# A decoder layer's feed-forward stage: where the vector engine adds a tile's sum, and where it takes the first half's maximum

## The chip, the cores and the metric

The kernel runs on one core of a Trainium2 chip. The core has a matrix engine (TensorE, PE), a vector engine (VectorE, DVE), a scalar engine (ScalarE, ACT), a general engine (GpSimd, POOL) and a queue engine that mostly issues transfers (SyncE, SP). Each engine works through its own list of instructions in order, and the lists meet only through semaphores. The metric is the device time of one execution in microseconds (us), the median of several runs; lower is better.

## What is computed

The program is one decoder layer on 2,048 tokens of width 512: windowed attention, a four-expert mixture that routes by token id, and a feed-forward stage with quantized activations. The change touches the feed-forward stage alone:

```python
def activation_quant(x):                       # per token, 8 bit
    s = 127 / clip(max(abs(x), axis=-1), EPS)
    return clip(round(x * s), -128, 127) / s
def bit_linear(x, w):                          # weight_quant(w): -1, 0 or 1, times mean(abs(w))
    return activation_quant(x) @ weight_quant(w).T
h = silu(bit_linear(x, w_gate)) * bit_linear(x, w_up)     # 2048 columns
h = rms_norm(h, ln_weight)
out = x_residual + bit_linear(h, w_down)                  # x is layernorm(x_residual)
```

## The kernel before, in words

The feed-forward stage, `ffn_phase`, works on 16 tiles of 128 tokens. The 2,048 hidden columns of a tile are four chunks of 512 (c = 0 to 3), and two chunks are a half. For tile t the work is this:

- TensorE, `gate_up(t, c)`: four matmuls into `gate_ps` and four into `up_ps`. Both exist twice and alternate by chunk.
- ScalarE, `gate_of(t, c)`: the silu, `f_gate` from `gate_ps`.
- VectorE, `hidden(t, c)` (line 1606): the h values of the chunk, from `up_ps` and `f_gate`. Here they are called h0 to h3.
- GpSimd, `weighted(t, c)` (line 1473): `hw`, which is h times the norm's weight. Here hw0 to hw3.
- VectorE, `top_of(t, n)` (line 1612): the largest absolute value of a half of `hw` in each row. `top_of(t, 0)` needs hw0 and hw1, `top_of(t, 1)` needs hw2 and hw3.
- ScalarE, `squares(t, n)` (line 1537): sum of squares of a half of h. VectorE `sum_squares` and GpSimd `rms_of` make the norm's factor of it.
- VectorE `scale_h(t)` (lines 1625 to 1634) and `quantize_h(t)` (line 1643, two halves, `hq_big`), then ScalarE `pack(t, 0)` and `pack(t, 1)` (line 1522, `hq`), then SyncE transposes each half by a DMA into `hqT` (line 1429).
- TensorE, `down(t, g)` for g = 0 to 3 (line 1738): four matmuls each, all sixteen adding up in the single buffer `f_y_ps`.
- VectorE, `y_of(t)` (line 1648): scales the finished `f_y_ps` and adds it to the tile's residual. SyncE stores the result and loads a later tile in its place.

These steps are spread over several passes of one loop. In its pass t, TensorE runs `gate_up(t, c)` and behind each of them `down(t - 2, c)`, since `LATE_DOWN` is 2. `down(t, 0)` waits for `y_of(t - 1)`, because `f_y_ps` exists once. `gate_up(t, 3)` waits for h1 of tile t, `gate_up(t + 1, 0)` for h2, `gate_up(t + 1, 1)` for h3. ScalarE's pass t is: second half's squares of tile t - 1, gate 0, normalize tile t + 2, gate 1, copy of the transposed x, pack 0 of tile t - 1, gate 2, pack 1 of tile t - 1, gate 3, first half's squares of tile t. GpSimd's pass t is `rms_of(t - 1)`, hw0, hw1, hw2, `rstd_of(t + 3)`, hw3, and a small scale.

VectorE's pass t, written out by hand at lines 1665 to 1688, is: `mean_of(t + 2)` (line 1580, one short instruction), `y_of(t - 3)`, `top_of(t - 1, 1)`, h0, the norm and quantizer of tile t - 1 with the maximum of x for tile t + 2 between them, h1, h2, `quantize_x(t + 2)`, statistics of tile t + 3 (lines 1568 to 1575), `top_of(t, 0)`, h3. What is left of the last tiles follows the loop.

Of the kernel before, what the change touches and what calls it, by code (L numbers as in the profile page):

```python
# [53 lines left out]
LATE_DOWN = 2  # L54
# [1278 lines left out]
def ffn_phase(nc, io, x2, y, sh):  # L1333
# [4 lines left out]
    with ExitStack() as ctx:  # L1338
# [69 lines left out]
        def inside(t):  # L1408
            return 0 <= t < TILES

        def flat(tile, i):
            return tile[:, i].rearrange("p c n -> p (c n)")

        with nc.Block() as block:
# [149 lines left out]
            def _(dve):  # L1564
                def stats_of(t):
                    i = t % 2
                    dve.wait_ge(x_loaded[t % len(homes)], t // len(homes) * 16 + 16)
                    nc.vector.bn_stats(bn_st[:, i, :], xt[t]).then_inc(stats_step, 1)  # L1568

                def variance_of(t):  # L1570
                    i = t % 2
                    dve.wait_ge(stats_step, t + 1)
                    nc.vector.bn_aggr(bn_mv[:, i, :], bn_st[:, i, :]).then_inc(stats_done, 1)  # L1573
                    dve.wait_ge(stats_done, t + 1)
                    nc.vector.tensor_scalar(var_eps[:, i:i + 1], bn_mv[:, i, 1:2], LN_EPS, None, ALU.add).then_inc(eps_added, 1)

                def mean_of(t):
                    i = t % 2
                    dve.wait_ge(rstd_ready, t + 1)
                    nc.vector.scalar_tensor_tensor(mean_rstd[:, i:i + 1], bn_mv[:, i, 0:1], -1.0, rstd[:, i:i + 1],  # L1580
                                                   ALU.mult, ALU.mult).then_inc(mean_ready, 1)

                def top_of_x(t):
                    dve.wait_ge(xn_ready, t + 1)
                    nc.vector.tensor_reduce(x_max[:], xn[:], AX.X, ALU.max, apply_absolute_value=True).then_inc(xq_step, 1)  # L1585

                def scale_x(t):
                    at = t * XQ_STEPS
                    dve.wait_ge(xq_step, at + 1)
                    if inside(t - 1):  # L1590
                        dve.wait_ge(gu_ready, t)
                    nc.vector.tensor_scalar(x_max127[:], x_max[:], Q_EPS, 1.0 / QMAX, ALU.max, ALU.mult).then_inc(xq_step, 1)  # L1592
                    dve.wait_ge(xq_step, at + 2)
                    nc.vector.reciprocal(x_inv[:], x_max127[:]).then_inc(xq_step, 1)

                def quantize_x(t):
                    dve.wait_ge(xq_step, (t + 1) * XQ_STEPS)
                    if inside(t - 1):
                        dve.wait_ge(xq_transposed, t)
                    nc.vector.tensor_scalar(xq_big[:], xn[:], x_inv[:], CODE, ALU.mult, ALU.add).then_inc(xq_ready, 1)  # L1600

                def hidden(t, c):
                    i = t % 2
                    dve.wait_ge(gate_ready, t * FC + c + 1)
                    dve.wait_ge(up_summed, t * FC + c + 1)
                    nc.vector.scalar_tensor_tensor(h[:, i, c, :], up_ps[c % 2][:], gu_scale[:, i, 1:2], gate[:, c % 2, :],  # L1606
                                                   ALU.mult, ALU.mult).then_inc(h_ready, 1)

                def top_of(t, n):
                    i = t % 2  # L1610
                    dve.wait_ge(hw_ready, t * FC + 2 * n + 2)
                    nc.vector.tensor_reduce(hw_max[:, i, n:n + 1], flat(hw, i)[:, n * HALF:n * HALF + HALF], AX.X, ALU.max,  # L1612
                                            apply_absolute_value=True).then_inc(hw_max_ready, 1)

                def sum_squares(t):
                    dve.wait_ge(sq_ready, (t + 1) * HALVES)
                    nc.vector.tensor_reduce(h_ss[:], h_sq[:, t % 2, :], AX.X, ALU.add).then_inc(ss_ready, 1)
                    dve.wait_ge(ss_ready, t + 1)
                    nc.vector.tensor_scalar(h_var[:], h_ss[:], 1.0 / F, RMS_EPS, ALU.mult, ALU.add).then_inc(h_var_ready, 1)

                def scale_h(t):
                    i = t % 2
                    at = t * HQ_STEPS
                    dve.wait_ge(hw_max_ready, (t + 1) * HALVES)
                    nc.vector.tensor_reduce(h_top[:], hw_max[:, i, :], AX.X, ALU.max).then_inc(hq_step, 1)
                    dve.wait_ge(hq_step, at + 1)
                    dve.wait_ge(rms_ready, t + 1)
                    nc.vector.tensor_scalar(h_max[:], h_top[:], h_rms[:], Q_EPS, ALU.mult, ALU.max).then_inc(hq_step, 1)  # L1628
                    dve.wait_ge(hq_step, at + 2)
                    nc.vector.reciprocal(h_inv[:], h_max[:]).then_inc(hq_step, 1)  # L1630
                    nc.vector.tensor_scalar(y_scale[:, t % (LATE_DOWN + 2):t % (LATE_DOWN + 2) + 1], h_max[:], w_mean[:, 2:3], 1.0 / QMAX, ALU.mult, ALU.mult)\
                        .then_inc(hq_step, 1)
                    dve.wait_ge(hq_step, at + 4)
                    nc.vector.tensor_scalar(h_mul[:], h_inv[:], h_rms[:], QMAX, ALU.mult, ALU.mult).then_inc(hq_step, 1)  # L1634

                def quantize_h(t):
                    i = t % 2
                    dve.wait_ge(hq_step, (t + 1) * HQ_STEPS)
                    for n in range(HALVES):
                        cols = slice(n * HALF, n * HALF + HALF)  # L1640
                        if inside(t - 1):
                            dve.wait_ge(hq_packed, (t - 1) * HALVES + n + 1)
                        nc.vector.tensor_scalar(hq_big[:, cols], flat(hw, i)[:, cols], h_mul[:], CODE, ALU.mult, ALU.add)\  # L1643
                            .then_inc(hq_ready, 1)

                def y_of(t):
                    dve.wait_ge(y_summed, t + 1)
                    nc.vector.scalar_tensor_tensor(xt[t], y_ps[:], y_scale[:, t % (LATE_DOWN + 2):t % (LATE_DOWN + 2) + 1], xt[t],  # L1648
                                                   ALU.mult, ALU.add).then_inc(y_ready, 1)
# [15 lines left out]
                for t in range(TILES):  # L1665
                    if inside(t + 2):
                        mean_of(t + 2)
                    if inside(t - 1 - LATE_DOWN):
                        y_of(t - 1 - LATE_DOWN)
                    if inside(t - 1):  # L1670
                        top_of(t - 1, 1)
                    hidden(t, 0)
                    if inside(t - 1):
                        sum_squares(t - 1)
                    if inside(t + 2):
                        top_of_x(t + 2)
                        scale_x(t + 2)
                    if inside(t - 1):
                        scale_h(t - 1)
                        quantize_h(t - 1)  # L1680
                    hidden(t, 1)
                    hidden(t, 2)
                    if inside(t + 2):
                        quantize_x(t + 2)
                    if inside(t + 3):
                        stats_of(t + 3)
                        variance_of(t + 3)
                    top_of(t, 0)
                    hidden(t, 3)
                last = TILES - 1  # L1690
                y_of(last - LATE_DOWN)
                top_of(last, 1)
                sum_squares(last)
                scale_h(last)
# [125 lines left out]
```

## Time and profile before

| | us |
|---|---|
| median of 3 runs | 809.09 |
| lowest, highest | 807.49, 811.71 |
| the profiled execution's own time | 808.96 |
| its span | 807.1 |
| busy in the span: TensorE | 740.2 |
| VectorE | 590.4 |
| ScalarE | 473.2 |
| GpSimd | 281.0 |

The profiled execution's time is 1.86 us more than its span, which lies around the span. The feed-forward stage begins at about 600 us of the span and ends with it; its first h value starts at 611.4. TensorE's end times are modelled, so its busy time is not a measure of how much room it has. Two starts of an engine's consecutive instructions tell its pace better.

### The profile page before, as it was taken

Reading aid. Unit: us, or ns where it says so; the run is one execution under the profiler, and the core shown is the slowest. Engines: PE = TensorE matmul, PEld = TensorE weight load, DVE = VectorE, ACT = ScalarE, POOL = GpSimd, SP = SyncE. Lnnn points to the kernel's source line nnn. Section 1 sums busy time; section 2 is a strip of 40 time slices with the busy share of each in tenths; the row PEclk is TensorE's granted clock in tenths of the full one; section 3 lists DMA queues with packets and bytes.
Section 4 is the critical chain, followed back from the end, with each engine's and each line's share of the span. In section 5 each row is a group of like instructions: output and inputs, shape, how many; then the busy total and the mean of one; then the engine's idle time right before and its main releaser. Section 6 shows DMA issues by size and latency. Waiting matters only on the chain. (4 is left out here: it accounts for less than half of the span.)

```text
span 807.1 us, 14098 instructions
## 1 busy us (share of the span) xinstructions
PE 740.2 (92%) x5150; PEld 507.8 (63%) x5150; DVE 590.4 (73%) x1092; ACT 473.2 (59%) x1025; POOL 281.0 (35%) x282
## 2 busy tenths in 40 slices
PE   5988999999999999999978789999957899999997
PEld 4756777777777777777655568888833343434443
DVE  6886666877668866677675467778628888888875
ACT  5555676666666666677555144444415766767674
POOL 2011213223042130314455234443214555555552
PEclk9998999999999999999989899999989999999999
DMA  9200031113121040313210375553122232433332
GB/s 312 107 1 28 27 105 37 45 54 131 52 81 54 28 157 27 106 30 129 105 53 2 95 274 176 201 199 137 46 82 85 52 85 73 105 91 73 73 78 79
DMA packets 56482, 74.12 MB, mean 92 GB/s; under 512 B 35615, under 2 KB 37663, under 8 KB 54752
## 3 DMA queue, kind: packets, MB, share of 16 engines
q1 hardware_dynamic: 50672, 56.17, 22.8%
q0 software_dynamic: 5456, 16.53, 5.9%
q8 instruction: 43, 0.70, 0.4%
q10 hardware_dynamic: 288, 0.52, 0.2%
q14 instruction: 23, 0.19, 0.1%
HBM read 52.71 MB, written 13.39 MB: 82 GB/s over the span
## 5 line engine op out<-in xcount | busy, mean ns | idle before, releaser
L527 ACT ACTIVATE probs<-s_ps,neg_max 128x512 f32<-128x512 f32 (+2 forms) x256 | 152.3, 610 | 19.5 <-DVE neg_max L696 18.1
L696 DVE TENSOR_REDUCE neg_max<-s_ps 128x2 f32<-128x1024 f32 (+2 forms) x128 | 124.5, 1014 | 33.6 <-PE s_ps L910 33.0
L930 PE MATMUL pT_ps<-ident,probs 128*128 128x128 f32 x832 | 115.6, 280 | 9.7 <-DVE probs L717 8.4
L539 ACT ACTIVATE probs<-pT_ps 128x512 f32<-128x512 f32 x96 | 57.4, 598 | 98.6 <-PE pT_ps L930 98.3
L930 PEld LDWEIGHTS pT_ps<-ident,probs 128*128 128x128 f32 x832 | 93.9, 144 | 25.2 <-DVE probs L717 11.2
L717 DVE COPY probs<-pT_ps 128x512 f32<-128x512 f32 x112 | 76.6, 684 | 36.8 <-PE pT_ps L930 36.5
L1473 POOL TENSOR_TENSOR hw<-h,ln_w_sb 128x512 f32<-128x512 f32 x64 | 83.2, 1310 | 52.3 <-DVE h L1606 52.3
L1738 PE MATMUL f_y_ps<-w_tern,hqT 128*128 128x512 bf16 x256 | 65.1, 379 | 11.8 <-DVE xn L1648 5.3
L1717 PE MATMUL gate_ps<-w_tern,xqT 128*128 128x512 bf16 x256 | 65.9, 380 | 8.3 <-DVE h L1606 7.4
L843 PE MATMUL side_ps<-w_hi 128*128 128x512 f32 x172 | 71.0, 413 | 0.0
L843 PE MATMUL side_ps<-w_hi,w_lo 128*128 128x512 f32 x172 | 67.3, 391 | 0.0
L843 PE MATMUL side_ps<-w_lo,w_hi 128*128 128x512 f32 x172 | 67.2, 391 | 0.0
L1717 PE MATMUL up_ps<-w_tern,xqT 128*128 128x512 bf16 x256 | 65.7, 379 | 0.0
L399 POOL TENSOR_TENSOR aT_hi<-norm,one_col 128x512 fp32r<-128x512 f32 x15 | 15.6, 1040 | 125.0 <-DVE norm L708 86.6
L1606 DVE SCALAR_TENSOR_TENSOR h<-up_ps,gu_scale,f_gate 128x512 f32<-128x512 f32 x64 | 47.7, 745 | 7.1 <-ACT f_gate L1529 7.0
L527 ACT ACTIVATION_READ_ACCUMULATOR probs<-s_ps,neg_max 128x1 f32 x256 | 52.8, 206 | 0.0
L952 PE MATMUL pv_ps<-probs,v_sb 128*32 128x256 f32 (+1 forms) x896 | 52.3, 369 | 0.2 <-ACT probs L539 0.2
L391 POOL TENSOR_TENSOR norm<-rinv,one_col 128x512 f32<-128x512 f32 x16 | 16.7, 1041 | 102.8 <-DVE rinv L703 102.8
L1717 PEld LDWEIGHTS gate_ps<-w_tern,xqT 128*128 128x128 bf16 x256 | 23.6, 98 | 42.0 <-DVE h L1606 15.4
L1738 PEld LDWEIGHTS f_y_ps<-w_tern,hqT 128*128 128x128 bf16 x256 | 23.2, 97 | 42.0 <-DMA hqT<-hq 18.0
L1522 ACT ACTIVATE hq<-hq_big,minus_offset 128x1024 bf16<-128x1024 f16 x30 | 34.3, 1143 | 25.4 <-DVE hq_big L1643 25.4
L1529 ACT ACTIVATE f_gate<-gate_ps,gu_scale 128x512 f32<-128x512 f32 x64 | 43.1, 674 | 8.2 <-PE gate_ps L1717 8.2
(247 smaller groups left out, 1635.5 us busy)
## 6 DMA issues: line engine op xcount, KB each, us to landing
w_piece<-w_ffn SPq DMA_DIRECT2D x24, 512.0 KB
w_stage<-w_ffn SPq DMA_DIRECT2D x12, 1024.0 KB
xres<-x POOLq DMA_DIRECT2D x4, 1024.0 KB, 5.7
xn<-x SPq DMA_DIRECT2D x12, 256.0 KB, 3.0
xn<-x SPq DMA_DIRECT2D x3, 1024.0 KB
x<-xres POOLq DMA_DIRECT2D x3, 1024.0 KB, 4.8
xn<-c SPq DMA_DIRECT2D x2, 1024.0 KB, 6.1
v_next<-c SPq DMA_DIRECT2D x2, 1024.0 KB, 6.0
```

The lines of the kernel that those rows point to most:

```text
L527: nc.scalar.activation(weights[qt][:, h, at:at + width(qt)], s_ps[:, h, 0:width(qt)], ACT.Exp, bias=neg_max[:, qt % 2, h:h + 1], accum_out ...
L539: nc.scalar.activation(out, turned_p, ACT.Identity).then_inc(slot_copied[0], 1)
L696: nc.vector.tensor_reduce(neg_max[:, qt % 2, 2 * s:2 * s + 2], s_ps[:, 2 * s:2 * s + 2, 0:width(qt)], AX.X, ALU.max, negate=True).then_inc ...
L717: nc.vector.tensor_copy(weights[qt][:, :, a:z], pT_ps[:, 1, :].rearrange("p (h n) -> p h n", h=GH))\
L843: last = nc.tensor.matmul(out, lt, r, start=(first and n == 0), stop=(final and n == len(terms) - 1))
L930: last = nc.tensor.transpose(pT_ps[:, k % 2, h * P:h * P + P], weights[qt][:, h, a:z], ident[:])
L952: last = nc.tensor.matmul(pv_ps[HD * h:HD * h + HD, to], v_sb[:, slot, f:f + HD], p, start=first, stop=final, tile_position=(0, HD * h))
L1473: nc.gpsimd.tensor_tensor(hw[:, t % 2, c, :], h[:, t % 2, c, :], ln_w[:, c * CHK:c * CHK + CHK], ALU.mult)\
L1529: nc.scalar.activation(gate[:, c % 2, :], gate_ps[c % 2][:], ACT.Silu, scale=gu_scale[:, t % 2, 0:1])\
L1606: nc.vector.scalar_tensor_tensor(h[:, i, c, :], up_ps[c % 2][:], gu_scale[:, i, 1:2], gate[:, c % 2, :], ALU.mult, ALU.mult).then_inc(h_re ...
L1717: last = nc.tensor.matmul(out[:], xqT[:, t % 2, k, :], weights[:, k, cols], start=(k == 0), stop=(k == DK - 1))
L1738: last = nc.tensor.matmul(y_ps[:], hqT[:, t % 2, k, :], down_w[:, k, :], start=(k == 0), stop=(k == FK - 1))
```

## The change

Two calls move in VectorE's list, and nothing else. `y_of`, which stood behind `mean_of` at the head of the next pass, now stands right behind h3 at the end of the pass (`y_of(t - 2)` in pass t is the same tile's sum as `y_of(t - 3)` in pass t + 1). `top_of(t, 0)`, which stood ahead of h3, now stands in pass t + 1, behind `mean_of` and directly ahead of `top_of(t, 1)`. Every semaphore, buffer and instruction stays as it was.

```diff
                 for t in range(TILES):
                     if inside(t + 2):
                         mean_of(t + 2)
-                    if inside(t - 1 - LATE_DOWN):
-                        y_of(t - 1 - LATE_DOWN)
                     if inside(t - 1):
+                        top_of(t - 1, 0)
                         top_of(t - 1, 1)
                     hidden(t, 0)
...
                         stats_of(t + 3)
                         variance_of(t + 3)
-                    top_of(t, 0)
                     hidden(t, 3)
+                    if inside(t - LATE_DOWN):
+                        y_of(t - LATE_DOWN)
                 last = TILES - 1
-                y_of(last - LATE_DOWN)
+                top_of(last, 0)
                 top_of(last, 1)
                 sum_squares(last)
                 scale_h(last)
```

VectorE's list between two passes in the steady part is shown first, as one piece of the difference. `hw_max` is what `top_of` writes, `h` is h3 and then the next tile's h0, `mean_rstd` is `mean_of`, `xn<-f_y_ps` is `y_of`.

```order
 L1573 BN_AGGR f_bn_mv<-f_bn_st 128x2
 L1575 TENSOR_SCALAR f_var_eps<-f_bn_mv 128x1
-L1612 TENSOR_REDUCE hw_max<-hw 128x1
-L1606 SCALAR_TENSOR_TENSOR h<-up_ps,gu_scale,f_gate 128x512
-L1580 SCALAR_TENSOR_TENSOR mean_rstd<-f_bn_mv,f_rstd 128x1
+L1606 SCALAR_TENSOR_TENSOR h<-up_ps,gu_scale,f_gate 128x512
 L1648 SCALAR_TENSOR_TENSOR xn<-f_y_ps,y_scale,xn 128x512
-L1612 TENSOR_REDUCE hw_max<-hw 128x1
+L1580 SCALAR_TENSOR_TENSOR mean_rstd<-f_bn_mv,f_rstd 128x1
+L1612 TENSOR_REDUCE hw_max<-hw 128x1 x2
 L1606 SCALAR_TENSOR_TENSOR h<-up_ps,gu_scale,f_gate 128x512
 L1617 TENSOR_REDUCE h_ss<-h_sq 128x1
```

The first maximum went from ahead of h3 to behind `mean_of`, so both maxima now stand together, and the sum follows h3 without `mean_of` between.

The second place is the end of VectorE's list, the last tile. Before, from its h1 on:

```order
L1606 SCALAR_TENSOR_TENSOR h<-up_ps,gu_scale,f_gate 128x512 x2
L1612 TENSOR_REDUCE hw_max<-hw 128x1
L1606 SCALAR_TENSOR_TENSOR h<-up_ps,gu_scale,f_gate 128x512
L1648 SCALAR_TENSOR_TENSOR v_next<-f_y_ps,y_scale,v_next 128x512
L1612 TENSOR_REDUCE hw_max<-hw 128x1
L1617 TENSOR_REDUCE h_ss<-h_sq 128x1
L1619 TENSOR_SCALAR h_var<-h_ss 128x1
```

After, from the same h1 on:

```order
L1606 SCALAR_TENSOR_TENSOR h<-up_ps,gu_scale,f_gate 128x512 x3
L1648 SCALAR_TENSOR_TENSOR v_next<-f_y_ps,y_scale,v_next 128x512
L1612 TENSOR_REDUCE hw_max<-hw 128x1 x2
L1617 TENSOR_REDUCE h_ss<-h_sq 128x1
L1619 TENSOR_SCALAR h_var<-h_ss 128x1
```

Here h1, h2 and h3 stand in a row with nothing between h2 and h3, since the last tiles have no statistics to take for later ones. TensorE, ScalarE, GpSimd and SyncE have the same lists before and after.

## Rows read from the trace of the kernel before

**Rows 1.** Busy time in one stretch: us, TensorE, weight loads, VectorE, ScalarE, GpSimd, clock, DMA share.

```profile
660.00:807.10 147.10, 132.08 (x635) 57.75 (x633) 120.98 (x268) 96.01 (x141) 73.36 (x78) 1.00 0.35 83
```

**Rows 2.** Timeline, VectorE: start, us, what, [idle before <- releaser]; tiles 8 and 9.

```profile
711.71 1.21 DVE L1612 TENSOR_REDUCE hw_max<-hw 128x1 f32<-128x1024 f32 x1
712.83 0.74 DVE L1606 SCALAR_TENSOR_TENSOR h<-up_ps,gu_scale,f_gate 128x512 f32<-128x512 f32 x1
713.49 0.15 DVE L1580 SCALAR_TENSOR_TENSOR mean_rstd<-f_bn_mv,f_rstd 128x1 f32<-128x1 f32 x1
713.56 0.74 DVE L1648 SCALAR_TENSOR_TENSOR v_next<-f_y_ps,y_scale,v_next 128x512 f32<-128x512 f32 x1
714.96 1.22 DVE L1612 TENSOR_REDUCE hw_max<-hw 128x1 f32<-128x1024 f32 x1 [0.66 <-POOL hw L1473]
716.09 0.74 DVE L1606 SCALAR_TENSOR_TENSOR h<-up_ps,gu_scale,f_gate 128x512 f32<-128x512 f32 x1
...
721.50 0.75 DVE L1606 SCALAR_TENSOR_TENSOR h<-up_ps,gu_scale,f_gate 128x512 f32<-128x512 f32 x1 [0.47 <-ACT f_gate L1529]
...
723.59 1.21 DVE L1612 TENSOR_REDUCE hw_max<-hw 128x1 f32<-128x1024 f32 x1
```

**Rows 3.** Timeline, GpSimd: hw3 of tile 8, then hw1, hw2 and rstd in tile 9.

```profile
713.65 1.27 POOL L1473 TENSOR_TENSOR hw<-h,ln_w_sb 128x512 f32<-128x512 f32 x1 [1.24 <-DVE h L1606]
...
721.11 2.68 POOL L1473 TENSOR_TENSOR hw<-h,ln_w_sb 128x512 f32<-128x512 f32 x2 [2.17 <-DVE h L1606]
723.75 0.55 POOL L1460 TENSOR_TENSOR f_rstd<-f_var_eps,f_minus_half 128x1 f32<-128x1 f32 x1
```

**Rows 4.** Timeline, ScalarE: gate 0 of tile 9, pack 1 of tile 8, gate 3 of tile 9.

```profile
714.66 0.67 ACT L1529 ACTIVATE f_gate<-gate_ps,gu_scale 128x512 f32<-128x512 f32 x1
...
721.37 1.14 ACT L1522 ACTIVATE hq<-hq_big,minus_offset 128x1024 bf16<-128x1024 f16 x1
722.41 0.68 ACT L1529 ACTIVATE f_gate<-gate_ps,gu_scale 128x512 f32<-128x512 f32 x1
```

**Rows 5.** Timeline, TensorE: pass 9, its down 0, down 2, gate 3, up 3, down 3.

```profile
714.45 1.02 PE L1738 MATMUL f_y_ps<-w_tern,hqT 128*128 128x512 bf16 x4 [0.75 <-DVE v_next L1648]
...
719.85 1.03 PE L1738 MATMUL f_y_ps<-w_tern,hqT 128*128 128x512 bf16 x4
721.09 1.04 PE L1717 MATMUL gate_ps<-w_tern,xqT 128*128 128x512 bf16 x4 [0.22 <-DVE h L1606]
721.96 1.03 PE L1717 MATMUL up_ps<-w_tern,xqT 128*128 128x512 bf16 x4
722.83 1.03 PE L1738 MATMUL f_y_ps<-w_tern,hqT 128*128 128x512 bf16 x4
```

**Rows 6.** Timeline, the first tile: its pack 1 and the first matmuls that read `hqT`.

```profile
626.30 1.14 ACT L1522 ACTIVATE hq<-hq_big,minus_offset 128x1024 bf16<-128x1024 f16 x1
...
630.64 1.04 PE L1738 MATMUL f_y_ps<-w_tern,hqT 128*128 128x512 bf16 x4 [0.99 <-DMA hqT<-hq]
```

**Rows 7.** Timeline, VectorE in the first tile, where there is no sum yet: h3, second maximum.

```profile
617.77 0.74 DVE L1606 SCALAR_TENSOR_TENSOR h<-up_ps,gu_scale,f_gate 128x512 f32<-128x512 f32 x1
...
619.89 1.22 DVE L1612 TENSOR_REDUCE hw_max<-hw 128x1 f32<-128x1024 f32 x1 [1.31 <-POOL hw L1473]
```

**Rows 8.** Timeline, tiles 13 to 15: TensorE's down 3, VectorE's h0 behind it (last: `h_ss`).

```profile
770.37 1.03 PE L1738 MATMUL f_y_ps<-w_tern,hqT 128*128 128x512 bf16 x4
...
774.52 0.74 DVE L1606 SCALAR_TENSOR_TENSOR h<-up_ps,gu_scale,f_gate 128x512 f32<-128x512 f32 x1
...
781.20 1.03 PE L1738 MATMUL f_y_ps<-w_tern,hqT 128*128 128x512 bf16 x4
...
785.03 0.74 DVE L1606 SCALAR_TENSOR_TENSOR h<-up_ps,gu_scale,f_gate 128x512 f32<-128x512 f32 x1
...
791.65 1.03 PE L1738 MATMUL f_y_ps<-w_tern,hqT 128*128 128x512 bf16 x4
...
795.54 0.15 DVE L1617 TENSOR_REDUCE h_ss<-h_sq 128x1 f32<-128x2 f32 x1
```

## Prediction

> **What bounds the kernel now.** The change lies in the feed-forward stage, so I first read the busy times of its last 147.1 us [rows 1]. TensorE shows 132.08 and VectorE 120.98, both high, and TensorE's clock is granted in full (1.00, its 2.4 GHz level). Neither share tells which one sets the pace. For that I read the timelines of one tile on each engine.
>
> On VectorE the first maximum of tile 8 starts at 711.71 and that of tile 9 at 723.59, so a tile takes 11.88 us [rows 2]. The pattern holds over many tiles: the second maximum of tile 0 starts at 619.89 [rows 7], that of tile 8 at 714.96 [rows 2], eight steps of 11.88. In this cycle VectorE stands idle in two places only: 0.66 us ahead of the second maximum, released by GpSimd's hw, and 0.47 us ahead of h2, released by ScalarE's gate [rows 2]. All else in its cycle is its own work. TensorE's stops in the same cycle end with VectorE: 0.75 us until `y_of` has freed `f_y_ps`, and 0.22 us until h1 is done [rows 5]. So VectorE's list sets the pace, with two loans to others in it, and whatever shortens that list's cycle shortens the stage, until TensorE has no room left.
>
> The first of the two idle times is made by the order. h3 starts at 712.83, GpSimd can begin hw3 only when it is done (713.65) and takes 1.27 us [rows 3], while VectorE has just `mean_of` and `y_of` to do (713.49 and 713.56) before it needs hw3.
>
> **What the change moves, in a steady tile.** I work forward from 723.59, where VectorE stands behind the statistics in tile 9. Before, from that point to the next h0 is 716.09 - 711.71 = 4.38 us [rows 2].
>
> Now h3 stands first. Its inputs are there: gate 3 ends at 722.41 + 0.68 = 723.09 [rows 4], and the up matmuls at 721.96 + 1.03 = 722.99 [rows 5]. So h3 starts at 723.59, 1.12 us earlier than it would have. Then:
> - `y_of`, 0.66 us after it (712.83 to 713.49 is what an h value holds the engine), at 724.25. It waits for the last down matmuls, which end at 722.83 + 1.03 = 723.86 [rows 5]. With 0.08 us for the hand-over (h3's end at 713.57 to hw3's start at 713.65 [rows 2, 3]) they are there at 723.94. This wait cost nothing before, with 1.4 us to spare; now 0.31 us are left.
> - `mean_of`, 0.67 us later (`y_of` has the shape and the 0.74 us of an h value), at 724.92. It needs rstd, which GpSimd ends at 723.75 + 0.55 = 724.30 [rows 3].
> - the first maximum, 0.07 us later (713.49 to 713.56), at 724.99. hw0 and hw1 are long done.
> - the second maximum, 1.12 us later (711.71 to 712.83), at 726.11. It needs hw3. GpSimd is free at 724.30, h3 ends at 724.33, so hw3 runs from 724.41 to 725.68. The first maximum now lies over this work, and 0.43 us are to spare. The 0.66 us of idling are gone.
> - h0 of tile 10, 1.13 us later (714.96 to 716.09), at 727.24. Gate 0 follows the squares of the second half: it started 1.83 us after h3 and ended at 2.50 [rows 2, 4], so it ends at 726.09 and h0 does not wait.
>
> That is 0.66 + 0.67 + 0.07 + 1.12 + 1.13 = 3.65 us instead of 4.38: **0.73 us a tile**, and the cycle becomes 7.50 (716.09 to 723.59) + 3.65 = 11.15 us. The other idle time, 0.47 us ahead of h2, stays: quantize, pack 0, gate 2 and h2 keep their distances.
>
> **What is late next.** TensorE must follow a cycle of 11.15. Its down 0 no longer waits for `y_of`, which ends at 724.99. Its own work lets it start at 722.83 + 3 x 0.87 = 725.44 (0.87 is one group of four matmuls, 721.96 to 722.83 [rows 5]). But the transposed `hqT` may not have landed. The trace of before shows that wait bare once, at the first tile: from pack 1's start at 626.30 to the matmuls at 630.64 are 4.34 us [rows 6]. Pack 1 starts at 721.37 here [rows 4], so down 0 starts at 725.71, 0.27 us late. From down 0 to the end of down 2 TensorE needs 719.85 + 0.87 - 714.45 = 6.27 us [rows 5], so it reaches gate 3 at 731.98. That one waits for h1 in any case, until 721.09 + 11.15 = 732.24. So 0.26 us are left, and the late transpose costs nothing. SyncE's queue isn't touched: its transposes hang on the packs, and its store of a sum only finds that sum ready earlier.
>
> TensorE's own work in a cycle is those 6.27 us and the five groups behind them (gate 3, up 3, down 3, the next tile's gate 0 and up 0), 5 x 0.87: 10.62 us in 11.15. It has some 0.5 us left.
>
> A rule of the Trainium skill bears on this room. "Perfetto Trace Analysis", in "Identifying the Most-Contended Engine", says that the matmul busy share does not measure TensorE's headroom and that the weight loads' busy share should be used for it. By that, TensorE would be at 57.75 / 147.1 = 39% here and could never become the bound; the distances of the starts say 10.62 of 11.15 us, 95%. The sum is the same by both, but by the page the rival in which TensorE takes over would have no chance. I go by the rows and keep it.
>
> **The first and the last tiles.** Behind tiles 0 and 1 there is no sum to add, and the second maximum waits longer, 1.31 us, at 2.12 us behind h3 [rows 7]. With h3 earlier by the maximum's 1.12 us, the first maximum fits into those 2.12 us (0.66 + 0.07 + 1.12 = 1.85), and the second still waits for hw3 at the same distance. So these two steps gain the full 1.12 us each: 2.24.
>
> Steps 2 to 12 (behind tile 2 to behind tile 12) are the steady ones: 11 x 0.73 = 8.03.
>
> Tiles 13, 14 and 15 have no statistics ahead of h3, and before, the first maximum filled the time until gate 3 was done. Now h3 and then `y_of` wait for TensorE: `y_of` starts when down 3 has ended, its start + 1.03 + 0.08, and from there to the next h0 are 0.67 + 1.12 + 1.13 = 2.92. Tile 13: 770.37 + 1.11 + 2.92 = 774.40 against 774.52, a gain of 0.12. Tile 14: 781.20 + 4.03 = 785.23 against 785.03, a loss of 0.20. Tile 15: 791.65 + 4.03 = 795.68 against 795.54, a loss of 0.14 [rows 8]. Together -0.22. The hand-over of 0.08 is taken at its long end; at 0 the three give +0.02.
>
> **The sum**: 2.24 + 8.03 - 0.22 = 10.05 us. The profiled execution took 808.96, so it would take 798.91; the median of the runs lies 0.13 above it, which gives 799.0.
>
> **Rivals.**
> 1. A new wait eats part of it. The likely one is `y_of`: if down 3 ends later than I think, `y_of` stops VectorE with `mean_of`, both maxima and the next h0 queued behind it, where before the first maximum stood ahead. It is covered by 0.31 us directly, and by another 0.26 us at gate 3. If the transpose and TensorE together run 1.0 us later than worked out, 0.43 us a tile is lost, 4.7 in all: 803.7. Against it: each distance above was measured in this very loop. For it: both margins are narrow, and the transpose's landing is seen bare only in the first tile [rows 6].
> 2. TensorE takes over and the time stays. If TensorE's modelled ends hide work, so that its cycle cannot fall below 11.6 to 11.9 us, the steady tiles give 0 to 0.3 us each and what is left is at most the first two: 804 to 809, with 807 in the middle. For it: the highest busy share. Against it: both its stops have a VectorE releaser.
> 3. Slower. `hqT` lands later once TensorE runs closer behind it. Down 3 is late with it, and VectorE stops at `y_of`. The loss passes the gain when the landing is later by more than 0.26 + 0.31 + 0.73 = 1.30 us; each 0.1 us beyond it costs 1.1 us. At 1.8 us late: 11 x 0.5 = 5.5 us, 814.6. Against it: the change moves no transfer relative to the packs, and the landing behind pack 1 was measured with TensorE already waiting for it [rows 6].
> 4. The wait on hw3 stays, because GpSimd's multiply runs slower beside the maximum. It may take 0.43 us more before it shows; the pair hw1 and hw2 takes 2.68 us beside other VectorE work, 1.34 each against 1.27 [rows 3]. At most some 0.07 to 0.2 us, which is hidden: the forecast holds.
>
> **Chances.** The forecast with its cover as worked out (797.9 to 800.5): 0.73. A part of the gain (rival 1, 800.5 to 804.9): 0.13. Within 0.5% (805.0 to 813.1, rival 2): 0.09. Slower: 0.03. More than forecast: 0.02, since I see no second idle time that would close. The 0.5% bound is 4.0 us, about what a measurement of this kernel can tell from no change. Faster by more than that: 0.88, same 0.09, slower 0.03. The range must also hold the spread of medians, since the three runs of before lie 4.2 us apart: 796.5 to 803.0.
>
> **What the profile of after would show.** In a steady tile the second maximum follows the first after 1.12 us with no idle from GpSimd; VectorE's only idle is 0.47 us at h2; the cycle is 11.15 us. TensorE's wait at down 0 ends with the transpose and is 0.3 us instead of 0.75 on `y_of`; the stop at gate 3 is near 0.1. hw3 lasts 1.27 us. In tiles 14 and 15 `y_of` is preceded by idle time released by TensorE. It would be wrong if `y_of` shows idle time in the steady tiles, if TensorE shows no stop at all and the cycle is over 11.3, or if the transpose lands more than 4.4 us behind pack 1's start.

## The result, and the profile after

The changed kernel takes 807.3 us in the median of 22 runs, the kernel before 809.56 us in 22 runs beside it. The ratio is 0.9976 with a 95% interval of 0.9965 to 0.9987: about 2 us faster, where 10 were forecast. The profiled execution of after took 806.35 us with a span of 804.5.

VectorE's timeline between tiles 9 and 10 answers to rows 2 (start, us, what, [idle before <- releaser]):

```profile
721.18 0.75 DVE L1606 SCALAR_TENSOR_TENSOR h<-up_ps,gu_scale,f_gate 128x512 f32<-128x512 f32 x1
721.85 0.74 DVE L1648 SCALAR_TENSOR_TENSOR v_next<-f_y_ps,y_scale,v_next 128x512 f32<-128x512 f32 x1
722.51 0.79 DVE L1580 SCALAR_TENSOR_TENSOR mean_rstd<-f_bn_mv,f_rstd 128x1 f32<-128x1 f32 x1
723.22 2.33 DVE L1612 TENSOR_REDUCE hw_max<-hw 128x1 f32<-128x1024 f32 x2
725.48 0.74 DVE L1606 SCALAR_TENSOR_TENSOR h<-up_ps,gu_scale,f_gate 128x512 f32<-128x512 f32 x1
```

Almost all is as forecast. `y_of` follows h3 after 0.67 us and waits for nothing, both maxima run without a gap, and the idle time ahead of the second maximum is gone. One row is not: `mean_of`, one column wide, takes 0.79 us, where it took 0.15 [rows 2]. From its start to the next is 0.71 us instead of 0.07. From h3 to the next h0 are 4.30 us, not 3.65.

The lost time is booked as the instruction's own duration. It appears in no list of waits, and nothing stands idle. The line of `mean_of` in the two kernels (count: shortest/median/longest ns, first and last start), first before, then after:

```profile
L1580 DVE SCALAR_TENSOR_TENSOR mean_rstd<-f_bn_mv,f_rstd x16: 147/149/161, 604.5 to 761.0; 128x1 f32<-128x1 f32 x16
```

```profile
L1580 DVE SCALAR_TENSOR_TENSOR mean_rstd<-f_bn_mv,f_rstd x16: 149/792/795, 604.1 to 757.9; 128x1 f32<-128x1 f32 x16
```

GpSimd's timeline in the same stretch of after, which answers to rows 3:

```profile
721.34 0.54 POOL L1460 TENSOR_TENSOR f_rstd<-f_var_eps,f_minus_half 128x1 f32<-128x1 f32 x1
722.01 1.27 POOL L1473 TENSOR_TENSOR hw<-h,ln_w_sb 128x512 f32<-128x512 f32 x1
723.24 0.20 POOL L1468 TENSOR_TENSOR gu_scale<-w_mean,x_max 128x2 f32<-128x2 f32 x1
```

rstd, for which `mean_of` waits by semaphore, is done at 721.88, 0.63 us before `mean_of` starts. But hw3 runs from 722.01 to 723.28, and `mean_of` ends at 723.30. That is the first theory, L: `mean_of` reads two tensors from SBUF (`f_bn_mv` and `f_rstd`), and such a VectorE instruction is held while GpSimd works on its own SBUF operands. h and `y_of` have one tensor in PSUM and one in SBUF, and the maxima read one tensor, so by L they would be free of it. This timeline hardly tests that: `y_of` starts ahead of hw3, the maxima 0.06 us before its end. But h2 of before starts 0.39 us into hw1 and takes its usual 0.75 us [rows 2, 3], and a maximum inside hw3 keeps its 1.21 us (e2 below).

**Where the 10 us went.** From the h0 starts of both timelines:

| | forecast gain | in the profiles |
|---|---|---|
| two first steps | 2.24 | 9.65 -> 8.55 and 11.88 -> 11.36: 1.62 |
| eleven steady steps | 8.03 | 130.73 -> 129.81: 0.92 |
| tiles 13 to 15 | -0.22 | 0.18 - 0.31 + 0.00: -0.13 |
| stage begins earlier | - | 0.21 |
| sum | 10.05 | 2.62 |

The steady step is 11.80 us instead of 11.15. The 0.64 us by which `mean_of` overran, eleven times, are 7.0 us of the 7.4 missing. The second tile is another 0.60 short, and about 0.3 came back at the end and by the earlier start. In the second tile h3 waited for TensorE, whose clock stood at half (1.2 GHz) from 625.4 to 628.8 us of the span. Four matmuls took 1.91 us there instead of 1.03. First TensorE, then VectorE in after:

```profile
624.71 1.27 PE L1717 MATMUL gate_ps<-w_tern,xqT 128*128 128x512 bf16 x4 [2.30 <-DVE h L1606]
625.77 1.91 PE L1717 MATMUL up_ps<-w_tern,xqT 128*128 128x512 bf16 x4
```

```profile
627.79 0.75 DVE L1606 SCALAR_TENSOR_TENSOR h<-up_ps,gu_scale,f_gate 128x512 f32<-128x512 f32 x1 [0.50 <-PE up_ps L1717]
```

### The profile page after: what moved, and what is told of

It is laid out like the page before. It is cut to its first block and busy times, and to the rows that moved or that the text cites. A ratio compares the mean times of both kernels' runs of the same rounds, so it can differ in the third digit from the quotient of the medians.

```text
span 804.5 us, 14098 instructions
## 1 busy us (share of the span) xinstructions
PE 740.3 (92%) x5150; PEld 507.6 (63%) x5150; DVE 594.6 (74%) x1092; ACT 473.8 (59%) x1025; POOL 281.9 (35%) x282
## 5 line engine op out<-in xcount | busy, mean ns | idle before, releaser
L930 PE MATMUL pT_ps<-ident,probs 128*128 128x128 f32 x832 | 113.9, 277 | 10.4 <-DVE probs L717 9.1
L930 PEld LDWEIGHTS pT_ps<-ident,probs 128*128 128x128 f32 x832 | 92.7, 142 | 25.5 <-DVE probs L717 11.8
L1717 PEld LDWEIGHTS up_ps<-w_tern,xqT 128*128 128x128 bf16 x256 | 25.3, 99 | 30.8 <-issue 1.1
```

What stands on the lines that cost most here:

```text
L930: last = nc.tensor.transpose(pT_ps[:, k % 2, h * P:h * P + P], weights[qt][:, h, a:z], ident[:])
L1717: last = nc.tensor.matmul(out[:], xqT[:, t % 2, k, :], weights[:, k, cols], start=(k == 0), stop=(k == DK - 1))
```

## The experiments

Four explanations of the 0.71 us were set against each other. **L**: held by GpSimd, because two tensors are read from SBUF. **B**: it comes from standing right behind the sum. **S**: any one-column instruction behind a long one pays it. **T**: TensorE is the bound at 11.8, and the 0.79 only fill a wait. The trace of after already speaks against T, since TensorE itself stands still for VectorE's h1 at gate 3, for 0.80 us where near 0.1 was forecast:

```profile
718.67 1.04 PE L1717 MATMUL gate_ps<-w_tern,xqT 128*128 128x512 bf16 x4 [0.80 <-DVE h L1606]
```

Each experiment's time is a median, and its ratio is to runs of before taken beside it. Besides each total I give the steady step (h0 to h0) and the stage from h0 of tile 1 to the last `h_ss`, which leaves out that the stage begins up to 5 us sooner or later from one profile to the next. That stretch is 174.52 us before and 173.21 after. Steps and stage come from one profile of each kernel. The steady steps of one profile mostly agree within some hundredths of a microsecond, while the ratios of e1 to e4 have overlapping intervals. So the steps carry the argument, and the totals only confirm its direction.

**The maximum alone (e1).** `y_of` goes back behind `mean_of`; both maxima stay together.

```diff
 for t in range(TILES):
     if inside(t + 2):
         mean_of(t + 2)
+    if inside(t - 1 - LATE_DOWN):
+        y_of(t - 1 - LATE_DOWN)
     if inside(t - 1):
         top_of(t - 1, 0)
         top_of(t - 1, 1)
...
     hidden(t, 3)
-    if inside(t - LATE_DOWN):
-        y_of(t - LATE_DOWN)
 last = TILES - 1
+y_of(last - LATE_DOWN)
 top_of(last, 0)
```

> Only the first maximum moves; the sum stays behind mean_of, so VectorE runs h3, mean_of, sum, both maxima. Theory L (mean_of reads two tensors in SBUF and is held while GpSimd's multiply hw3 runs): mean_of starts as soon as rstd is there, about 0.72 us behind h3's start, and hw3 begins at 0.83, so mean_of comes first, lasts 0.15 us, and the step is 11.2 us a tile; total about 9 us under before (0.989). If it came 0.1 us later it would be held for all of hw3 and the step would be near 12.2. Rival B (the 0.79 us come from standing right behind the sum, whatever GpSimd does): mean_of isn't behind the sum, 0.15 us, step 11.2. Rival T (TensorE is the bound at 11.8): step 11.8.

798.85 us, ratio 0.9897 (0.9863 to 0.9931); step 11.24, stage 166.45. So half of the change, alone, is worth 8.1 us of the stage, and the whole of it 1.3 (in medians 10.3 and 2.3). VectorE's timeline:

```profile
726.67 0.75 DVE L1606 SCALAR_TENSOR_TENSOR h<-up_ps,gu_scale,f_gate 128x512 f32<-128x512 f32 x1
727.41 0.16 DVE L1580 SCALAR_TENSOR_TENSOR mean_rstd<-f_bn_mv,f_rstd 128x1 f32<-128x1 f32 x1
727.48 0.74 DVE L1648 SCALAR_TENSOR_TENSOR xn<-f_y_ps,y_scale,xn 128x512 f32<-128x512 f32 x1
```

`mean_of` starts 0.74 us behind h3, some hundredths late for rstd and just ahead of hw3 (0.83 us behind h3 in after), and lasts 0.16. T falls: TensorE follows a step of 11.24. B and L both allow this.

**mean_of between the maxima (e2).** The order of after, with `mean_of` one place later.

```diff
-if inside(t + 2):
-    mean_of(t + 2)
 if inside(t - 1):
     top_of(t - 1, 0)
+if inside(t + 2):
+    mean_of(t + 2)
+if inside(t - 1):
     top_of(t - 1, 1)
```

> The kernel after, with mean_of moved behind the first maximum, where GpSimd's hw3 should just have ended (2.10 us behind h3's start against 2.45). Theory L: mean_of lasts 0.15 us, the step is 11.15 us, total about 9.5 us under before (0.988). Rival B: mean_of is no longer behind the sum, also 11.15. Rival T: 11.8. Rival S (a one-column instruction behind any long one drains it): mean_of still about 0.8 and 11.8.

801.53 us, ratio 0.9903 (0.9866 to 0.9940); step 11.15 to 11.16, stage 165.81. Its VectorE, then its GpSimd:

```profile
717.47 0.74 DVE L1648 SCALAR_TENSOR_TENSOR v_next<-f_y_ps,y_scale,v_next 128x512 f32<-128x512 f32 x1
718.12 1.21 DVE L1612 TENSOR_REDUCE hw_max<-hw 128x1 f32<-128x1024 f32 x1
719.25 0.15 DVE L1580 SCALAR_TENSOR_TENSOR mean_rstd<-f_bn_mv,f_rstd 128x1 f32<-128x1 f32 x1
719.32 1.21 DVE L1612 TENSOR_REDUCE hw_max<-hw 128x1 f32<-128x1024 f32 x1
```

```profile
717.63 1.27 POOL L1473 TENSOR_TENSOR hw<-h,ln_w_sb 128x512 f32<-128x512 f32 x1
```

Behind a long instruction, but after hw3's end at 718.90, `mean_of` lasts 0.15 us. S falls. The step is the forecast 11.15: with `mean_of` out of hw3, the other terms of the steady step were right. The stage gains 8.71 us and the first step, which lies ahead of it, 1.10, together 9.8 of the 10.05 forecast. The medians show 7.6 (801.53 against 809.12), less than the 9.5 expected; the five runs lie from 797.24 to 802.07.

**mean_of with one tensor (e3).** Order as in after; the same value by another form of instruction.

```diff
-nc.vector.scalar_tensor_tensor(mean_rstd[:, i:i + 1], bn_mv[:, i, 0:1], -1.0, rstd[:, i:i + 1],
-                               ALU.mult, ALU.mult).then_inc(mean_ready, 1)
+nc.vector.tensor_scalar(mean_rstd[:, i:i + 1], bn_mv[:, i, 0:1], rstd[:, i:i + 1], -1.0,
+                        ALU.mult, ALU.mult).then_inc(mean_ready, 1)
```

> The kernel after in its own order, only the form of mean_of changed: a tensor_scalar with one tensor input and rstd as a per-row scalar, the same value. It still stands behind the sum and beside hw3. Theory L: it is not held, 0.15 to 0.22 us, step 11.15 to 11.25, total about 9 us under before. Rival B and S: it still takes about 0.79 us, step 11.8, total as the kernel after. Rival T: 11.8 with TensorE without a stop.

799.90 us, ratio 0.9887 (0.9841 to 0.9932); step 11.20 to 11.21, stage 166.96. VectorE, then GpSimd:

```profile
720.50 0.74 DVE L1648 SCALAR_TENSOR_TENSOR v_next<-f_y_ps,y_scale,v_next 128x512 f32<-128x512 f32 x1
721.16 0.20 DVE L1580 TENSOR_SCALAR mean_rstd<-f_bn_mv,f_rstd 128x1 f32<-128x1 f32 x1
721.28 1.21 DVE L1612 TENSOR_REDUCE hw_max<-hw 128x1 f32<-128x1024 f32 x1
```

```profile
720.67 1.27 POOL L1473 TENSOR_TENSOR hw<-h,ln_w_sb 128x512 f32<-128x512 f32 x1
```

In the same place, right behind the sum and inside hw3, it takes 0.20 us. B falls. So does the thought that the time is spent on rstd's semaphore, for which this form waits as well. What counts for `mean_of` is the second tensor operand; with rstd as a per-row scalar it isn't held. The other form of instruction alone doesn't explain it, since h2 has the old form and keeps its length beside hw1.

**hw3 in two instructions (e4).** Order and form as in after.

```diff
-nc.gpsimd.tensor_tensor(hw[:, t % 2, c, :], h[:, t % 2, c, :], ln_w[:, c * CHK:c * CHK + CHK], ALU.mult)\
-    .then_inc(hw_ready, 1)
+for lo, hi in ((0, CHK // 2), (CHK // 2, CHK)) if c == 3 else ((0, CHK),):
+    last = nc.gpsimd.tensor_tensor(hw[:, t % 2, c, lo:hi], h[:, t % 2, c, lo:hi],
+                                   ln_w[:, c * CHK + lo:c * CHK + hi], ALU.mult)
+last.then_inc(hw_ready, 1)
```

> The kernel after in its own order, only GpSimd's hw3 issued as two instructions of 256 columns. Theory L: mean_of (starts 1.33 us behind h3) is held until the first of them ends (about 1.5), so it lasts about 0.2 us instead of 0.79, step about 11.3, total about 8 us under before. Rival B and S: mean_of 0.79, step 11.8. Rival T: 11.8.

802.04 us, ratio 0.9908 (0.9877 to 0.9939); step 11.25 to 11.27 (one of 11.51), stage 167.05. VectorE, then GpSimd:

```profile
722.10 0.25 DVE L1582 SCALAR_TENSOR_TENSOR mean_rstd<-f_bn_mv,f_rstd 128x1 f32<-128x1 f32 x1
```

```profile
721.60 1.41 POOL L1474 TENSOR_TENSOR hw<-h,ln_w_sb 128x256 f32<-128x256 f32 x2
```

The two halves are shown as one row; taken as equal, the first ends near 721.60 + 0.71 = 722.31, and `mean_of` ends at 722.35. It is held to the end of the one GpSimd instruction that is running, not to the end of the one behind it.

**The sum alone (e5).** The first maximum stays ahead of h3, only the sum moves.

```diff
 if inside(t + 2):
     mean_of(t + 2)
-if inside(t - 1 - LATE_DOWN):
-    y_of(t - 1 - LATE_DOWN)
...
 top_of(t, 0)
 hidden(t, 3)
+if inside(t - LATE_DOWN):
+    y_of(t - LATE_DOWN)
```

> Only the sum moves: the first maximum stays ahead of h3, and VectorE runs maximum, h3, sum, mean_of, maximum. mean_of starts 1.33 us behind h3's start, inside hw3 (0.83 to 2.09), and the second maximum has to wait for hw3 until 2.12 in any case. Theory L: mean_of is held until hw3 ends and lasts about 0.78 us, but nothing else is delayed: the step stays 11.88 us and the time that of before. Rival (moving the sum is worth something by itself, because TensorE's down 0 gets f_y_ps sooner): mean_of as before, step under 11.8.

809.79 us, ratio 1.0009 (0.9991 to 1.0028); step 11.88 to 11.90, stage 174.54. VectorE, then GpSimd:

```profile
726.34 0.79 DVE L1580 SCALAR_TENSOR_TENSOR mean_rstd<-f_bn_mv,f_rstd 128x1 f32<-128x1 f32 x1
727.14 1.22 DVE L1612 TENSOR_REDUCE hw_max<-hw 128x1 f32<-128x1024 f32 x1
```

```profile
725.84 1.27 POOL L1473 TENSOR_TENSOR hw<-h,ln_w_sb 128x512 f32<-128x512 f32 x1 [1.23 <-DVE h L1606]
```

The hold is there (it ends at 727.13, hw3 at 727.11), but the second maximum would have waited for hw3 anyway. Moving the sum gains nothing and costs nothing, until the maximum is moved too. Then it costs 6.8 us of the stage (166.45 in e1 against 173.21).

**The hold made anew (e8).** e2 with an additional one-column instruction with two SBUF tensors, its result unused, beside hw2.

```diff
 stats_of(t + 3)
+nc.vector.scalar_tensor_tensor(scratch[:], x_max[:], -1.0, x_inv[:], ALU.mult, ALU.mult)
 variance_of(t + 3)
```

> The second kernel (mean_of between the maxima) with one more one-column instruction that reads two tensors in SBUF, written to a tile that nobody reads, right behind the statistics (bn_stats), where GpSimd runs hw2 and the sum is far away. Theory L: it is held until hw2 ends, about 0.5 us, and the step grows from 11.15 to about 11.6 us. Rival B (only behind the sum) and a plain cost: 0.07 us more, 11.2. Rival S (a one-column instruction behind any long one): 0.7 us, 11.8.

806.40 us, ratio 0.9957 (0.9940 to 0.9973); step 11.57 (one of 11.76), stage 171.07. VectorE, then GpSimd:

```profile
722.60 0.68 DVE L1569 BATCH_NORM_STATS2 f_bn_st<-v_next 128x6 f32<-128x512 f32 x1
723.21 0.62 DVE L1688 SCALAR_TENSOR_TENSOR scratch<-x_max,x_inv 128x1 f32<-128x1 f32 x1
723.75 0.17 DVE L1574 BATCH_NORM_AGGREGATE f_bn_mv<-f_bn_st 128x2 f32<-128x6 f32 x1
```

```profile
721.13 2.68 POOL L1474 TENSOR_TENSOR hw<-h,ln_w_sb 128x512 f32<-128x512 f32 x2 [2.17 <-DVE h L1607]
```

GpSimd's pair hw1 and hw2 ends at 723.81, the new instruction at 723.83. Thirteen of them cost 5.3 us of the stage (171.07 against 165.81). Another tensor pair, another place, the same hold: L stands.

**Gate 2 ahead of pack 0 (e6).** e2, and ScalarE no longer makes VectorE wait 0.47 us ahead of h2.

```diff
+gate_of(t, 2)
 if inside(t - 1):
     pack(t - 1, 0)
-gate_of(t, 2)
```

> The second kernel (mean_of between the maxima) and one more swap: ScalarE runs gate 2 ahead of pack 0, which takes away VectorE's 0.47 us of idle time ahead of h2. If VectorE's list is the bound down to its own work, the step falls from 11.15 to 10.68 us. If TensorE is the next bound (10.62 us of work, and its down 3 must end before the sum), the step is 10.7 to 10.85, with idle time of VectorE ahead of the sum or h3 released by TensorE. If my margins are wrong: 11.15 as before. Total about 14 us under before, 0.982 to 0.984.

800.46 us, ratio 0.9900 (0.9877 to 0.9923); step 11.15 to 11.16 (the first 11.34), stage 165.80. Missed: the idle time went, the gain did not come. VectorE, then GpSimd:

```profile
726.23 1.40 DVE L1606 SCALAR_TENSOR_TENSOR h<-up_ps,gu_scale,f_gate 128x512 f32<-128x512 f32 x2
727.55 1.06 DVE L1600 TENSOR_SCALAR xq_big<-f_xn,x_inv 128x512 f32<-128x512 f32 x1
```

```profile
727.05 2.69 POOL L1473 TENSOR_TENSOR hw<-h,ln_w_sb 128x512 f32<-128x512 f32 x2 [2.16 <-DVE h L1606]
```

h1 and h2 now follow without a gap, but `quantize_x` takes 1.06 us instead of 0.50 and ends 0.3 us behind hw1 (727.05 + 1.27 = 728.32). It looks like the same kind of hold, with one tensor read. What sets `quantize_x` apart is its pace: its quantizing sister `quantize_h` does 1,024 columns in 0.75 us, where a maximum needs 1.21. That the pace is the reason is argued, not tested. The idle time had hidden this one. In before,

```profile
722.17 0.50 DVE L1600 TENSOR_SCALAR xq_big<-f_xn,x_inv 128x512 f32<-128x512 f32 x1
```

starts only 0.2 us before hw1's end (721.11 + 1.27 = 722.38 [rows 3]) and also ends 0.3 us behind it, with its length all but unchanged.

**Matmuls in place of the missing ones (e7).** e6, with TensorE kept busy in the first two tiles.

```diff
 if inside(t - LATE_DOWN):
     down(t - LATE_DOWN, c)
+else:
+    for _ in range(DK):
+        nc.tensor.matmul(y_ps[:], ident[:], gate_w[:, 0, 0:D], start=True, stop=True)
```

> The kernel of e6, with sixteen matmuls of no use in each of the first two tiles, where the down matmuls are missing (their output is overwritten). In the kernels whose clock fell to half near 626 us, the second tile took 0.3 to 0.6 us longer. If TensorE's stops in the first two tiles let the clock fall, it stays at full and this kernel is 0.3 to 0.6 us faster than e6, or the same where e6 happened to keep its clock; if the extra matmuls delay gate 0 to gate 3, it is slower by up to 1 us.

800.84 us, ratio 0.9901 (0.9878 to 0.9924); stage 165.84. The clock kept its full level near 626 us in this profile, and fell to half for 3.4 us near 787 instead. In e6 it had fallen near 628. The tile-1 and tile-2 steps are 10.79 + 11.40 us against 10.86 + 11.34 in e6. The filler gained nothing there, and ahead of it the first tile's step grew from 8.54 to 10.05 us: h2 and h3 of the first tile waited 1.48 and 0.44 us for TensorE, which had the filler in its list. In other profiles in which the clock halved near this place, the tile-1 step took 10.75 us (e9) and 11.62 us (e3), so what such a fall costs in general stays open.

**quantize_x behind h1 (e9).** e6, and the held instruction starts before GpSimd can.

```diff
 hidden(t, 1)
-hidden(t, 2)
 if inside(t + 2):
     quantize_x(t + 2)
+hidden(t, 2)
```

> The kernel of e6 with VectorE's quantize_x moved from behind h2 to behind h1. In e6 quantize_x lasts 1.06 us instead of 0.50. Theory L: it is held too (a tensor_scalar with source and result in SBUF, at twice the pace of the other forms) until GpSimd's hw1 ends; directly behind h1 it starts 0.66 us after h1's start, before hw1 can (0.82), so it takes 0.4 to 0.5 us, and hw1 starts up to 0.4 us later instead. VectorE's work alone would give 10.7 us a tile; GpSimd's list (h1, hw1, hw2, rstd, hw3, then the second maximum) gives 10.9 to 11.0, so the step falls from 11.15 to about 10.95, total 1.5 to 2.5 us under e6. Rival (quantize_x takes 1.06 us because it follows h2 without a gap): it takes about 1 us behind h1 as well, and the step stays 11.15.

800.20 us, ratio 0.9886 (0.9867 to 0.9906); step 11.03 in the mean of ten (10.97 to 11.14; the one before them 11.45), stage 165.17. VectorE:

```profile
725.71 0.48 DVE L1600 TENSOR_SCALAR xq_big<-f_xn,x_inv 128x512 f32<-128x512 f32 x1
...
728.14 0.75 DVE L1606 SCALAR_TENSOR_TENSOR h<-up_ps,gu_scale,f_gate 128x512 f32<-128x512 f32 x1 [0.29 <-PE up_ps L1718]
```

GpSimd, then TensorE:

```profile
725.87 2.67 POOL L1473 TENSOR_TENSOR hw<-h,ln_w_sb 128x512 f32<-128x512 f32 x2 [2.17 <-DVE h L1606]
```

```profile
718.52 1.03 PE L1718 MATMUL up_ps<-w_tern,xqT 128*128 128x512 bf16 x4
719.87 1.04 PE L1739 MATMUL f_y_ps<-w_tern,hqT 128*128 128x512 bf16 x4 [0.32 <-DMA hqT<-hq]
```

`quantize_x` takes 0.48 us again, with nothing changed about it but its place, so the rival (a neighbour without a gap) falls. One part of the expectation did not come: hw1 was to start up to 0.4 us later. It starts 0.82 us behind h1 (725.05), as in e6, and the pair takes 2.67 us against 2.69. So in these rows the VectorE instruction that came first did not visibly hold GpSimd. The step fell by 0.12 of the 0.2 expected, and the reason isn't the one I gave: h3 now waits 0.2 to 0.3 us for TensorE, and TensorE's only stop is the one for the transposed `hqT`. The 0.32 us shown for it are reckoned from modelled ends. From start to start (718.52 to 719.87) the group behind which it waits takes 1.35 us instead of 0.87, 0.48 more. In the mean of the ten tiles the 11.03 us are 10.62 of work and 0.41 of this stop. In total time e9 and e6 can't be told apart: 0.3 us between the medians, where 1.5 to 2.5 were expected.

**rstd behind hw3 (e10).** e9, with 0.55 us out of GpSimd's chain. The first part of the edit is in GpSimd's list, the second in VectorE's.

```diff
-if inside(t + 3):
-    rstd_of(t + 3)
 weighted(t, 3)
+if inside(t + 3):
+    rstd_of(t + 3)
...
-if inside(t + 2):
-    mean_of(t + 2)
 if inside(t - 1):
     top_of(t - 1, 1)
+if inside(t + 2):
+    mean_of(t + 2)
```

> The kernel of e9 with GpSimd's rstd moved behind hw3 and mean_of moved behind the second maximum, where GpSimd runs nothing long. If GpSimd's list bounds e9, its 0.55 us for rstd leave the chain and the step falls by 0.1 to 0.2 us more, to 10.8 to 10.9, near TensorE's 10.62; total 1 to 2 us under e9. If TensorE's down 3 (the sum waits for it) or the later mean_of, which ScalarE's normalize step needs, takes over, the step is that of e9 or up to 0.2 us longer.

797.88 us, ratio 0.9855 (0.9833 to 0.9877); step 11.01 in the mean of ten, stage 165.14. The step is that of e9, and not the 10.8 to 10.9 that a bound by GpSimd's list would have given, so that list wasn't e9's bound. TensorE shows the same stop:

```profile
720.07 1.04 PE L1738 MATMUL f_y_ps<-w_tern,hqT 128*128 128x512 bf16 x4 [0.30 <-DMA hqT<-hq]
```

It has the lowest median of all kernels run here and beats both before and after. The lower total against e9 isn't explained by this stage, and the intervals of the two ratios meet.

## Why the prediction was wrong, point by point

- **VectorE's list sets the pace, and the order makes its first idle time.** Right. With the maxima together and `mean_of` out of hw3 the step is 11.15 us (e2), the number of the sum.
- **"`mean_of`, 0.67 us later at 724.92 ... the first maximum, 0.07 us later (713.49 to 713.56)".** This step failed. The 0.07 us come from a row in which GpSimd stood idle: hw3 started at 713.65, after `mean_of` had ended at 713.64 [rows 2, 3]. The change puts h3, and with it hw3, ahead of `mean_of`, and so moves it into GpSimd's instruction. I looked only at what it waits for by semaphore (rstd, 0.6 us to spare) and not at what runs beside it. From its start to the next instruction's are 0.71 us there (after), 0.07 outside (e2), 0.12 with one tensor (e3), 0.18 with hw3 in two (e4). 11 x 0.64 = 7.0 us. None of the prediction's signs of being wrong looked at an instruction's length; the one that came near was a cycle over 11.3, but it was tied to a TensorE without a stop.
- **`y_of` has 0.31 us to spare; down 0 waits 0.27 us for the transpose; 0.26 us are left at gate 3.** Right. In e2 `y_of` never waits in the steady tiles, down 0 starts 0.24 us later than TensorE's own pace would let it (728.91 + 0.87 to 730.02), and gate 3 waits for h1 by 0.16 us. The margins are as narrow as said: in e9, 0.12 us a tile further on, they are gone.
- **The maximum hides hw3, with 0.43 us to spare.** Right. In e2 hw3 ends at 718.90 and the second maximum starts at 719.32, and hw3 keeps its 1.27 us beside the sum and the first maximum.
- **First tiles 2.24 us.** 1.10 for the first step, as worked out; 0.52 instead of 1.12 for the second, where TensorE ran at half clock and h3 waited 0.50 us for it. In e1, whose clock stayed full, that step took 10.78 us, 1.10 less than before.
- **Last tiles -0.22.** -0.13. `y_of` starts when down 3 has ended, as forecast, 0.03 to 0.04 us behind it instead of 0.08, and the next h0 follows 2.92 us later, as worked out. The long waits stand one instruction ahead of it, at h3: for gate 3 in tiles 13 and 15 (0.45 and 0.86 us), for TensorE in tile 14, the longest:

```profile
778.70 0.75 DVE L1606 SCALAR_TENSOR_TENSOR h<-up_ps,gu_scale,f_gate 128x512 f32<-128x512 f32 x1 [1.16 <-PE up_ps L1717]
```

- **The rivals.** None of the four was the one that came. The second comes nearest in its time (804 to 809) and has the wrong cause. In e9 and e10 TensorE and its wait for the transposed `hqT` set the step, at 11.0 us a tile and not at 11.6 to 11.9. The wait leads back through the packs to VectorE's quantizer, so TensorE alone is not shown to be the bound. The fourth looked for GpSimd made slower by VectorE; it was VectorE that was held by GpSimd. The price of its opposite was never asked for, and 0.88 for a clear gain was too sure for a sum that rested on every instruction keeping its length beside new neighbours.
- **The Trainium skill.** By its weight-load measure TensorE had 60% to spare. The runs side with the starts of the matmuls: 10.62 us of TensorE's work lie in a step of 11.03 (e9). The same rule of the Trainium skill, "Perfetto Trace Analysis", in "Identifying the Most-Contended Engine", names a second measure beside the weight loads, the matmul work done against the peak rate. The prediction left it out, so its "no chance" rested on half of the rule.

A rule that I had not weighed bears on it directly. The Trainium skill, "SBUF — State Buffer", in "Who interferes with whom", says that a VectorE instruction with two SBUF inputs contends with a GpSimd instruction that reads SBUF, and so does one in a 2-port mode. There whichever issues first has the shared ports for its whole length while the other is blocked. A `tensor_reduce` on trn2 never contends. The runs agree where GpSimd comes first: `mean_of` ends 0.02 us behind hw3, `quantize_x` is held in e6, and the maxima keep their 1.21 us. Where VectorE comes first they agree that `quantize_x` isn't held (e9), but show no blocked GpSimd: hw1 starts within `quantize_x` and the pair keeps its 2.67 us. No run shows which mode `quantize_x` was in.

## What to carry to other kernels

Before an instruction is moved, look at what runs on GpSimd at its new place: a VectorE instruction with two SBUF tensors, however small, can wait there for a whole GpSimd instruction, and everything in VectorE's list waits behind it. Price a moved instruction from a row with the same neighbours, or bound it by the neighbour's full length. A hold of this kind shows as a long duration and never as idle time, so compare the shortest and the longest time of each line. The cures seen here are to place it just ahead of the GpSimd instruction (e1, e9) or behind it (e2), or, for a one-column instruction, to give it a form with one tensor (e3). One tensor alone is no safeguard: `quantize_x` reads one and was held.

## What the runs showed of the hardware that I had not expected

- One column is enough to be held until the GpSimd instruction ends: 0.79 us instead of 0.15 (after, e5), 0.62 us in e8. The same value by `tensor_scalar` with a per-row scalar takes 0.20 us beside the same GpSimd instruction (e3).
- The order of the starts decides. `quantize_x` takes 1.06 us when it comes 0.5 us after hw1's start (e6), and 0.48 us when it comes just before it (e9). GpSimd's pair of instructions keeps its length either way.
- Removing an idle time can uncover a hold of the same size. In e6 h2 follows h1 after 0.66 us instead of 1.22, 0.56 us sooner, and `quantize_x` is 0.56 us longer, so the step stayed at 11.15 us.
